# A mixer and expert kernel whose output product C takes two matmuls instead of three, with its side work placed at other units

## The reference, cut to what matters

```python
x = x + _layernorm(attn(_layernorm(x)))      # mixer
x = x + _layernorm(ffn(_layernorm(x)))       # experts
# attn: Bu = u @ B_w.T                 (64 states)
#       h  = real part of the causal convolution of Bu with eig**t, |eig| = 1
#       y  = h @ C_w.T + D * u
# ffn:  g, u = x @ w_gate[e], x @ w_up[e]     (8 experts, 128 -> 512)
#       out  = sum_e cw[e] * ((silu(g) * u) @ w_down[e])
#       cw   = softmax(x @ w_router) * softmax(x @ w_gating / 0.1), normed
```

## Time and profile before

| | us |
|---|---|
| median of 3 runs (lowest, highest) | 1149.61 (1148.16, 1149.87) |
| the profiled execution | 1147.37 |
| its span, first to last instruction | 1145.4 |
| PE busy | 1110.9 (97%) |
| DVE busy | 936.1 (82%) |
| ACT busy | 731.6 (64%) |
| POOL busy | 708.5 (62%) |

### The profile page before, as it was taken

One profiled execution on the slowest core, in us unless ns is written; L12 is line 12 of the kernel. 1 busy time (PEld: TensorE's weight loads), 2 busy tenths in 40 slices (PEclk: granted clock), 3 DMA queues, 4 the chain that ended last, 5 costly groups with the idle time before them and its releaser, 6 DMA issues.

```text
span 1145.4 us, 16858 instructions
## 1 busy us (share of the span) xinstructions
PE 1110.9 (97%) x4818; PEld 897.2 (78%) x4818; DVE 936.1 (82%) x1751; ACT 731.6 (64%) x1415; POOL 708.5 (62%) x900
## 2 busy tenths in 40 slices
PE   8998999999999999999999999999999999999997
PEld 4676787787877878787887877878777887888885
DVE  7778888787888978888887887978878887887865
ACT  6765666656666576666656666576666756666564
POOL 1587766648557475766748567575756748557453
PEclk9999999999999999999999999999999999999998
DMA  4430322213132222322213133222322313132110
GB/s 137 118 111 12 100 56 77 72 47 93 47 93 75 65 65 50 99 56 77 72 48 98 42 93 74 66 65 54 95 56 76 73 47 93 46 84 56 43 52 19
DMA packets 184588, 80.17 MB, mean 70 GB/s; under 512 B 126736, under 2 KB 162224, under 8 KB 184496
## 3 DMA queue, kind: packets, MB, share of 16 engines
q1 hardware_dynamic: 184496, 79.09, 26.2%
HBM read 59.40 MB, written 19.66 MB: 69 GB/s over the span
## 4 chain that ended last, share of the span: by engine, by line
PE 73%; POOL 14%; issue 7%; ACT 1%; DVE 1%; POOLq 0%; ACTq 0%; DVEq 0%
PE y L365 8%; PE g L367 8%; PE g L365 8%; PE g L366 8%; PE y L367 8%; PE y L366 8%; PE u L365 8%; PE u L367 7%; PE u L366 7%; POOL hid_lo L1285 6%; POOL acc L1292 2%; POOL mv L1236 1%; POOL rstd L1250 1%; ACT hid_hi L673 1%; PE m_ps L365 1%
## 5 line engine op out<-in xcount | busy, mean ns | idle before, releaser
L1285 POOL TENSOR_TENSOR hid_lo<-hid,hid_hi 128x512 fp32r<-128x512 f32 x255 | 335.3, 1315 | 363.5 <-ACT hid_hi L673 363.4
L983 DVE TENSOR_TENSOR hid<-gate,u 128x512 f32<-128x512 f32 x512 | 348.9, 682 | 188.6 <-ACT gate L667 163.9
L667 ACT ACTIVATE gate<-g 128x512 f32<-128x512 f32 x512 | 305.2, 596 | 299.2 <-PE g L367 298.9
L673 ACT ACTIVATE hid_hi<-hid 128x512 fp32r<-128x512 f32 x512 | 319.8, 625 | 38.3 <-DVE hid L983 36.4
L989 DVE TENSOR_TENSOR hid_lo<-hid,hid_hi 128x512 fp32r<-128x512 f32 x257 | 236.7, 921 | 0.1
L365 PE MATMUL y<-hid_hi,w_hi 128*128 128x512 f32 x512 | 201.6, 394 | 12.2 <-POOL hid_lo L1285 11.6
L365 PE MATMUL g<-xe_hi,w_hi 128*128 128x512 f32 x512 | 200.2, 391 | 4.5 <-POOL w_lo L1228 2.9
L365 PE MATMUL u<-xe_hi,w_hi 128*128 128x512 f32 x512 | 200.0, 391 | 2.4 <-DVE hid L983 2.4
L367 PE MATMUL g<-xe_hi,w_lo 128*128 128x512 f32 x512 | 199.4, 389 | 0.0
L367 PE MATMUL u<-xe_hi,w_lo 128*128 128x512 f32 x512 | 199.4, 389 | 0.0
L367 PE MATMUL y<-hid_hi,w_lo 128*128 128x512 f32 x512 | 199.4, 389 | 0.0
(11 more groups left out here) (223 smaller groups left out, 1165.1 us busy)
## 6 DMA issues: line engine op xcount, KB each, us to landing
cw_b<-cw_scratch SPq DMA_DIRECT2D x128, 256.0 KB, 3.4
x_sb<-x_in SPq DMA_DIRECT2D x16, 256.0 KB, 3.1
xn_scratch<-mix_t SPq DMA_DIRECT2D x60, 64.0 KB, 2.7
feat<-xn_scratch SPq DMA_DIRECT2D x15, 256.0 KB, 2.6
out_scratch<-acc_t SPq DMA_DIRECT2D x60, 64.0 KB, 1.9
ffn<-out_scratch SPq DMA_DIRECT2D x15, 256.0 KB, 2.7
x_out<-o_sb SPq DMA_DIRECT2D x15, 256.0 KB, 2.4
y_scratch<-mix_t SPq DMA_DIRECT2D x56, 64.0 KB, 1.9
```

The costliest lines, as they stand in the source:

```text
L667: nc.scalar.activation(gate[:, k % 2, :], g_ps[k % 2][:], ACT.Silu).then_inc(gate_ready, 1)
L673: nc.scalar.activation(hid_hi[:, k % RING, :], hid[:, k % RING, :], ACT.Copy).then_inc(hi_ready, 1)
L983: nc.vector.tensor_tensor(hid[:, k % RING, :], gate[:, k % 2, :], u_ps[k % 2][:], ALU.mult).then_inc(hid_ready, 1)
L1285: nc.gpsimd.tensor_tensor(hid_lo[:, k % RING, :], hid[:, k % RING, :], hid_hi[:, k % RING, :].bitcast(f32), ALU.subtract).then_inc(lo_pool, 1)
```

## The change

Three things change.

1. The product C. The state that goes into it is the sum of the cosine and the sine rows, and C's weights are the same for both halves. Now `leave` writes its products to PSUM (`m_ps`), ACT copies the 64 sine rows to `w_sin` on the lower partitions (`move_sines`, unit 23), and DVE adds the halves there (`fold`, unit 23). `hi_w` takes the high part of these 64 rows into the upper half of `act_hi`, `lo_w` writes their low part into its lower half, so one 128-row operand holds both. Two matmuls do it: C's high part (which stands twice, in both halves of the rows) times this operand, and C's low part with zeros in its lower 64 rows.
2. The tables. In `X_AT` the scalings go from units 7, 8 to 8, 9, `hi_x` from 15 to 16, `du` and `lo_x` from 16 to 17. In `Y_AT` `z_a`, `z_b` go from 9, 10 to 10, 11, and `residual` from 11 to 12. SP issues the store and the load of the mixer's input after the fourth expert's spread (e == 4) instead of the fifth.
3. Chunk 0. The softmax for chunk 0 is spread over units 1 to 6. Chunk 1's input is turned by PE into `n_ps` instead of going through DRAM, its mixer stages come three to four units earlier, chunk 2's come one unit earlier from `hi_x` to `enter`, and the weight splits run at units 3 to 22 instead of 5 to 25.

```diff
-X_AT = {..., "scale_x_a": 7, "scale_x_b": 8, ..., "hi_x": 15, "du": 16, "lo_x": 16, "bu": 18, ...
+X_AT = {..., "scale_x_a": 8, "scale_x_b": 9, ..., "hi_x": 16, "du": 17, "lo_x": 17, "bu": 18, ...
...
-LATE_SPLITS = (5, 7, 9, 11, 13, 15, 17, 18, 19, 21, 23, 25)
+LATE_SPLITS = (3, 4, 6, 8, 10, 12, 14, 16, 17, 18, 20, 22)
...
-                    if e == 5 and c + 2 < NCHUNK:
+                    if e == 4 and c + 2 < NCHUNK:
                         store_x_blocks(c + 2)
                         load_x_feat(c + 2)
...
-                exact(m_ps[:], proj_hi[:, P:P + D], proj_lo[:, P:P + D], act_hi[:], act_lo[:]).then_inc(mixed_ready, 1)
+                nc.tensor.matmul(m_ps[:], proj_hi[:, P:P + D], act_hi[:], start=True, stop=False)
+                nc.tensor.matmul(m_ps[:], proj_lo[:, P:P + D], act_hi[:], start=False,
+                                 stop=True).then_inc(mixed_ready, 1)
...
+            def mix_move_sines(c):
+                act.wait_ge(parts_ready, c)
+                nc.scalar.activation(w_sin[:], m_ps[NS:P, :], ACT.Copy).then_inc(sines_moved, 1)
...
-                nc.scalar.activation(act_hi[:], v_sb[:], ACT.Copy).then_inc(act_hi_ready, 1)
+                nc.scalar.activation(act_hi[0:NS, :], v_sb[0:NS, :], ACT.Copy).then_inc(act_hi_ready, 1)
...
-                nc.vector.tensor_tensor(v_sb[:], sum_sb[:], trig[:], ALU.mult).then_inc(w_ready, 1)
+                nc.vector.tensor_tensor(m_ps[:], sum_sb[:], trig[:], ALU.mult).then_inc(parts_ready, 1)
+
+            def mix_fold(c):
+                dve.wait_ge(sines_moved, c)
+                nc.vector.tensor_tensor(v_sb[0:NS, :], m_ps[0:NS, :], w_sin[:], ALU.add).then_inc(w_ready, 1)
...
-                nc.vector.tensor_tensor(act_lo[:], v_sb[:], act_hi[:].bitcast(f32), ALU.subtract).then_inc(act_lo_ready, 1)
+                nc.vector.tensor_tensor(act_hi[NS:P, :], v_sb[0:NS, :], act_hi[0:NS, :].bitcast(f32),
+                                        ALU.subtract).then_inc(act_lo_ready, 1)
```

More of the change, by code:

```diff
@@ L41 @@
 PIECES = WCOLS // F
-X_AT = {"load_x": 0, "stats_x": 4, "norm_x": 5, "scale_x_a": 7, "scale_x_b": 8, "block_x": 10, "hi_x": 15, "du": 16,
-        "lo_x": 16, "bu": 18, "enter": 19, "scan": 21, "leave": 22, "hi_w": 24, "lo_w": 25, "c": 27, "y": 28, "block_y": 30}
-Y_AT = {"stats_y": 6, "norm_y": 7, "z_a": 9, "z_b": 10, "residual": 11, "stats_x1": 14, "norm_x1": 15, "scale_x1_a": 18,
+X_AT = {"load_x": 0, "stats_x": 4, "norm_x": 5, "scale_x_a": 8, "scale_x_b": 9, "block_x": 10, "hi_x": 16, "du": 17,
+        "lo_x": 17, "bu": 18, "enter": 19, "scan": 21, "leave": 22, "move_sines": 23, "fold": 23, "hi_w": 24, "lo_w": 25, "c": 27, "y": 28, "block_y": 30}
@@ L47 @@
+Y_AT = {"stats_y": 6, "norm_y": 7, "z_a": 10, "z_b": 11, "residual": 12, "stats_x1": 14, "norm_x1": 15, "scale_x1_a": 18,
         "scale_x1_b": 19, "block_xe": 20, "hi_xe": 25, "lo_xe": 26, "logits": 28, "softmax": 29, "peak": 30, "silus": 31}
[L48 to L52, removed]
@@ L53 @@
-SECOND_X_AT = {"stats_x": 5, "norm_x": 6, "scale_x_a": 9, "scale_x_b": 10, "block_x": 12, "hi_x": 19, "du": 20, "lo_x": 20,
-               "bu": 21, "enter": 22, "scan": 22, "leave": 23, "hi_w": 25, "lo_w": 26, "c": 28, "y": 29, "block_y": 30}
+FIRST_X_AT = {"scale_x_a": 0, "scale_x_b": 1, "turn_x": 3, "hi_x": 4, "du": 4, "lo_x": 4, "bu": 6, "enter": 7, "scan": 7,
+              "leave": 8, "move_sines": 9, "fold": 9, "hi_w": 10, "lo_w": 10, "c": 12, "y": 13}
+FIRST_Y_AT = {"turn_y": 14, "stats_y": 14, "norm_y": 15, "z_a": 17, "z_b": 18, "residual": 19, "stats_x1": 20, "norm_x1": 21,
+              "scale_x1_a": 24, "scale_x1_b": 25, "turn_xe": 26, "hi_xe": 27, "lo_xe": 27, "logits": 28, "softmax": 29,
+              "peak": 30, "silus": 31}
@@ L55 @@
+SECOND_X_AT = {"stats_x": 5, "norm_x": 6, "scale_x_a": 9, "scale_x_b": 10, "block_x": 12, "hi_x": 18, "du": 19, "lo_x": 19,
+               "bu": 20, "enter": 21, "scan": 22, "leave": 23, "move_sines": 24, "fold": 24, "hi_w": 25, "lo_w": 26, "c": 28, "y": 29, "block_y": 30}
 OWN_AT = {"exps": 0, "products": 1, "weights": 2}
-FIRST_OWN_AT = {"exps": 1, "products": 1, "weights": 2}
+FIRST_OWN_AT = {"softmax": 1, "peak": 2, "silus": 3, "exps": 4, "products": 5, "weights": 6, "weigh": 10}
 FIN_AT = {"fin_turn": 7, "fin_stats": 12, "fin_norm": 13, "fin_a": 21, "fin_b": 22, "fin_add": 23}
@@ L141, in build @@
         mix_t, feat, y_tok = sb("mix_t", [P, SEQ]), sb("feat", [P, SEQ]), sb("y_tok", [P, NT, D])
+        w_sin = sb("w_sin", [NS, SEQ])
         proj_hi, proj_lo = sb("proj_hi", [P, P + D], f32r), sb("proj_lo", [P, P + D], f32r)
@@ L177, in build @@
         xn_ready, xn_turned = sem("xn_ready"), sem("xn_turned")
+        parts_ready, sines_moved = sem("parts_ready"), sem("sines_moved")
         act_hi_ready, act_lo_ready, du_ready = sem("act_hi_ready"), sem("act_lo_ready"), sem("du_ready")
@@ L267, in store_x_blocks @@
             def store_x_blocks(c):
-                sp.wait_ge(x_blocked, c)
-                if c > 1:
-                    sp.wait_ge(xt_loaded, 16 * (c - 1))
+                sp.wait_ge(x_blocked, c - 1)
+                if c > 2:
+                    sp.wait_ge(xt_loaded, 16 * (c - 2))
                 to_features(xn_dram, mix_t, x_stored)
             def load_x_feat(c):
-                sp.wait_ge(x_stored, STORED * c)
-                if c > 1:
+                sp.wait_ge(x_stored, STORED * (c - 1))
+                if c > 2:
                     sp.wait_ge(act_lo_ready, 2 * c - 3)
@@ L325, in body @@
                     load_x(c + 2)
-                if first:
-                    store_x_blocks(1)
                 store_cw(c, par)
-                if first:
-                    load_x_feat(1)
                 for e in range(E):
@@ L435, in mix_c, with first_turn_x @@
                 pe.wait_ge(act_lo_ready, 2 * c)
-                exact(m_ps[:], proj_hi[:, P:P + D], proj_lo[:, P:P + D], act_hi[:], act_lo[:]).then_inc(mixed_ready, 1)
+                nc.tensor.matmul(m_ps[:], proj_hi[:, P:P + D], act_hi[:], start=True, stop=False)
+                nc.tensor.matmul(m_ps[:], proj_lo[:, P:P + D], act_hi[:], start=False,
+                                 stop=True).then_inc(mixed_ready, 1)
+            def first_turn_x():
+                pe.wait_ge(xn_ready, 2)
+                pe.wait_ge(raw_read, 1)
+                turn(n_ps, lambda j: xn[:, j, :]).then_inc(xn_turned, 1)
             def first_turn_y():
                 pe.wait_ge(y_ready, 2)
-                pe.wait_ge(raw_read, 1)
                 turn(n_ps, lambda j: y_sb[:, j * P:(j + 1) * P]).then_inc(y_turned, 1)
@@ L530, in body @@
                             mix_c(m)
+                        if k == at.get("turn_x"):
+                            first_turn_x()
                         if k == at.get("turn_y"):
@@ L591, in mix_scale_x @@
                     if c == 2:
-                        act.wait_ge(x_blocked, 1)
+                        act.wait_ge(xn_turned, 2)
                 for j in tiles:
@@ L599, in mix_hi_x @@
             def mix_hi_x(c):
-                act.wait_ge(xt_loaded, 16 * c)
+                if c == 1:
+                    act.wait_ge(xn_turned, 2)
+                else:
+                    act.wait_ge(xt_loaded, 16 * (c - 1))
                 act.wait_ge(mixed_ready, c)
-                nc.scalar.activation(act_hi[:], feat[:], ACT.Copy).then_inc(act_hi_ready, 1)
+                src = n_ps if c == 1 else feat
+                nc.scalar.activation(act_hi[:], src[:], ACT.Copy).then_inc(act_hi_ready, 1)
             def mix_du(c):
@@ L608, in mix_du @@
                     act.wait_ge(y_blocked, c - 2)
-                nc.scalar.activation(y_sb[:], feat[:], ACT.Copy, scale=d_col[:]).then_inc(du_ready, 1)
+                src = n_ps if c == 1 else feat
+                nc.scalar.activation(y_sb[:], src[:], ACT.Copy, scale=d_col[:]).then_inc(du_ready, 1)
+            def mix_move_sines(c):
+                act.wait_ge(parts_ready, c)
+                nc.scalar.activation(w_sin[:], m_ps[NS:P, :], ACT.Copy).then_inc(sines_moved, 1)
             def mix_hi_w(c):
                 act.wait_ge(w_ready, c + 1)
-                nc.scalar.activation(act_hi[:], v_sb[:], ACT.Copy).then_inc(act_hi_ready, 1)
+                nc.scalar.activation(act_hi[0:NS, :], v_sb[0:NS, :], ACT.Copy).then_inc(act_hi_ready, 1)
             def mix_z(c, tiles):
@@ L630, in mix_scale_x1 @@
                     if 0 < c < NCHUNK - 1:
-                        act.wait_ge(x_blocked, c + 1)
+                        act.wait_ge(x_blocked, c)
                 for j in tiles:
@@ L718, in body @@
                         round_piece(n // PIECES, n % PIECES)
-                    if first and k == 1:
+                    if first and k == FIRST_OWN_AT["silus"]:
                         mix_silus(0)
-                    if c == 1 and k == 0:
-                        mix_silus(1)
                     for m, at in stages(c):
@@ L735, in body @@
                             mix_du(m)
```

(27 more changed lines are left out.)

## The result

| | before | after |
|---|---|---|
| median (lowest, highest), us | 1149.74 (1148.16, 1151.35), 4 runs | 1170.93 (1169.89, 1171.81), 4 runs |
| ratio to before, 95% interval | | 1.0184 (1.0166, 1.0202) |
| span of the profiled execution, us | 1145.4 | 1169.5 |
| PE busy, us | 1110.9 | 1110.7 |

What follows compares the result with a forecast made beforehand. PE, busy 97% of the span, was taken as the bound. On the profiled execution, 1147.4 - 3.4 - 5.7 + 13.4 + 18.9 + 0 gave 1170.6, stated as 1170.5 us, range 1141 to 1178.

Steps and rivals of the forecast that it cites:

- The residual on POOL: Chunks 1 to 14: the residual delays POOL's unit 13 `hid_lo`, PE loses 0.96 us each; 13.4 us lost.
- `lo_x` between `hid_lo` and POOL: Ahead of `bu`, chunks 1 to 13: `lo_x` waits out POOL's `acc`, 1.45 us each; 18.9 us lost.
- The late load: ACT's wait at `hi_x` for `feat` goes with the earlier store; 13 chunks, 5.7 us saved.
- The product C: One matmul less in each of 15 mixers, 3.4 us saved; `fold` and `move_sines` at unit 23 cost nothing.
- Chunk 0: In chunk 0, the wait for the last split becomes waits for `hid_lo`; 0 in sum, between 6.7 saved and 5 lost.
- Rival A: At `bu`: the residual costs its 0.96 us, but `lo_x` precedes `acc` or ends in time; 1153 us, chance 0.27.
- rival B: At unit 13: POOL's delay stays under 0.35 us, PE doesn't stop, savings stand alone; 1138.3 us, chance 0.16.

Runs made afterwards that it cites:

- the old chunk 0: The changed kernel with residual at unit 11 and `lo_x` at 16, but chunk 0 as in the kernel before: 1142.72 us, ratio to before 0.9951.
- the norms: The changed kernel with residual at 11, `lo_x` at 16, and `norm_x` 5 to 6, `norm_y` 7 to 8, `fin_norm` 13 to 17: 1124.71 us.

## Why the prediction was right

It said 1170.5 us and 1170.93 was measured; the profiled spans grew by 24.1 us where the sum has 23.2. The two waits, their places and what ends them came as forecast, and taking the two steps back gave 32.3 us, as much as the 13.4 + 18.9 of the sum. That it fits to the tenth is luck in part: the terms below are off by up to 1.6 us, some up and some down. Point by point:

- *The residual on POOL*: forecast 0.96 us at unit 16 in 14 chunks, 13.4 in all. The profile has 0.95 in each, and 0.08 besides in the matmul behind the wait, which the sum left out: 14.4 in all. POOL's `hid_lo` of unit 13 starts 34.59 us into the chunk where the working gives 34.56. Taking it back gave 12.0 us alone, mainly since the wait at `bu` grows by 0.18 a chunk when it goes.
- *`lo_x` between `hid_lo` and POOL*: forecast 1.45 us in 13 chunks, 18.9 in all; the profile has 1.30, 16.9 in all, and with the 0.08 behind each wait 17.9. The end of `lo_x` was forecast to 0.04 us (42.08 against 42.04 into the chunk). The term is 0.15 too large mainly since PE itself was free for `bu` 40.89 us into the chunk, not 40.72: half of this is the slower matmul after the wait at unit 16, and the working also set PE's arrival 0.05 too early (492.24 + 0.96 is 493.20, not 493.16).
- *The late load*: forecast 5.7 us; alone it gave 5.9.
- *The product C*: forecast 3.4 us; alone it gave 1.8 (0.8 to 2.9 by the interval). "I cost them at nothing" holds in the regular chunks and fails in the chunk 0 of the kernel before, where the longer chain of chunk 1's mixer reaches PE.
- *Chunk 0*: forecast 0 within -6.7 and +5, measured +1.0. This was luck: C adds to chunk 0, the rearrangement takes about 2 off, and the profiled execution of the changed kernel lost some 1.4 us there at half clock, which the sum did not have. The wait there of 2.7 us for a `hid_lo` of POOL in place of the last split had been named; a wait of 1.5 us ahead of chunk 2's `bu`, the same turn-taking as in the regular chunks (`lo_x` issued at 79.26 behind a `hid_lo`, 1.77 us, with POOL's weight split waiting), had not.
- Rival A (`lo_x` slips in) fell with the rows of DVE and POOL after, rival B with the wait at unit 16. What rival A's premise, a free turn for `lo_x`, would have been worth is shown by the run with `acc` at unit 18: 0.25 us left at `bu` and 1157.21 us, inside A's 1151.7 to 1158 though not near its 1153.

## What to carry to other kernels

Before a step is moved, lay the timeline of the engine that runs it beside the deadlines of what stands behind it: a share of 62% busy did not tell it here, since POOL had 1.5 us to spare one step ahead and 0.35 us in the four units after. Where DVE and POOL both read two SBUF operands, count turns, not durations: two such DVE operations in a row give a waiting POOL operation a full turn between them. And when a bundle of edits comes out slower, take it apart by the place of each wait, since here 10 us of savings (1149.0 to 1138.6) lay under 32 us of losses (1138.6 to 1170.9), and two numbers of a table separated them.

## What the runs showed of the hardware

Six of the ten profiled executions have a stretch of 3.4 us in chunk 0 in which the granted clock is half (1.2 in place of 2.4 GHz): the changed kernel, `lo_x` at 16 alone, `acc` at 18, C alone, the early store and the old chunk 0. In the changed kernel it follows PE's wait of 2.7 us (columns: stretch, length, busy us of PE, PEld, DVE, ACT, POOL, granted clock, DMA):

```profile
86.00:91.80 5.80, 3.60 (x16) 2.63 (x15) 4.76 (x7) 3.53 (x7) 5.39 (x10) 1.00 0.00 0
91.80:95.20 3.40, 2.86 (x7) 2.31 (x8) 0.68 (x1) 0.69 (x2) 3.40 (x4) 0.50 0.00 0
95.20:100.00 4.80, 4.80 (x25) 3.96 (x24) 3.06 (x4) 3.52 (x8) 1.95 (x2) 1.00 0.02 5
```

PE's timeline in that stretch (start and duration in us, instruction, wait ahead of it):

```profile
92.34 0.76 PE L363 MATMUL y<-hid_hi,w_hi 128*128 128x512 f32 x1 [2.74 <-POOL hid_lo L1318]
...
93.76 0.63 PE L363 MATMUL g<-xe_hi,w_hi 128*128 128x512 f32 x1
94.18 0.63 PE L364 MATMUL g<-xe_lo,w_hi 128*128 128x512 f32 x1
```

Matmuls start 0.42 to 0.43 us apart there instead of 0.2265, which costs about 1.4 us in all. In the other profiles such a stretch cost 1.1 to 1.6 us.

The length of the wait alone does not decide it. At one place of chunk 0, the wait for the last weight split, the kernel before waited 2.95 us and kept the full clock, and with the early store the clock fell to half after 2.98 us. C alone and the old chunk 0 both wait 1.84 us for DVE's `hid` near the start; the clock fell at this place in the first and stayed in the second. At the wait for POOL's `hid_lo` the clock fell in all three profiles in which PE waited 2.7 us and stayed in all three with 2.5 (residual at 11, both steps back, the norms). These are single executions: what does decide it was not tried.

Executions of one kernel differ in this. In the 11 runs of C alone the mean granted clock goes from 0.997 down to 0.992 and the time from 1145.4 up to 1149.0 us with it. Their mean clock is 0.9952 against 0.9968 of the kernel before beside them, so a part of what C gives may be lost to the clock; no run separates it. A wait of PE thus cost up to 1.6 us more than its own length, in some executions.
